# Sixteen-head attention in a four-layer kernel: queries projected from split operands that are streamed by head, their parts made in the layer-0 feed-forward

## What is computed

```python
# layer 0, feed-forward: a router, a shared and an expert branch
shared_out = relu(x @ W_up.T) @ W_down.T
moe_out = sum(softmax(top2(x @ W_gate.T))) * (x @ W_expert)
# layer 2, attention: 16 heads of 128; x is 512 wide, the context 256
q = rmsnorm((x @ Wq).reshape(B, S, 16, 128)) * gq
k = rmsnorm((ctx @ Wk).reshape(B, S, 16, 128)) * gk
v = (ctx @ Wv).reshape(B, S, 16, 128)
attn = softmax(einsum("bqhd,bkhd->bhqk", q, k) / sqrt(128))
out = einsum("bhqk,bkhd->bqhd", attn, v).reshape(B, S, 2048) @ Wo
```

## Time and profile before

| | us |
|---|---|
| median of 3 runs | 3641.05 |
| lowest, highest | 3634.16, 3655.15 |
| the profiled execution, its own time | 3635.72 |
| its span | 3633.9 |

### The profile page before, as it was taken

How to read it: one execution, slowest core, us unless ns; L and a number is a source line. 1 busy time by engine, 2 the same in 40 slices (tenths; PEclk the granted TensorE clock), 3 DMA queues, 4 the chain that set the end, 5 groups by cost and what they waited for, 6 DMA issues and landing times. The chain is left out here.

```text
span 3633.9 us, 43465 instructions
## 1 busy us (share of the span) xinstructions
PE 3207.4 (88%) x14597; PEld 1930.8 (53%) x14628; DVE 2598.7 (72%) x3488; ACT 1806.3 (50%) x3413; POOL 1401.9 (39%) x956
## 2 busy tenths in 40 slices
PE   6868888999996888799999999999999878997995
PEld 2337644333333555455555555555555456785763
DVE  6864679877765888377777877777777755665786
ACT  4644333666663445355555556556655332664220
POOL 1121178000000000166666667766666634223540
PEclk9978999999998999899999999999999888998998
DMA  3026736222218100244544454445454345665311
GB/s 127 37 110 228 265 120 164 59 57 58 62 29 175 29 1 1 82 163 152 176 151 158 161 165 167 157 152 167 154 165 136 104 190 200 239 250 189 139 70 58
DMA packets 229735, 478.69 MB, mean 132 GB/s; under 512 B 36224, under 2 KB 69632, under 8 KB 213649
## 3 DMA queue, kind: packets, MB, share of 16 engines
q1 hardware_dynamic: 223280, 459.19, 39.2%
q0 software_dynamic: 6240, 16.81, 1.3%
HBM read 387.51 MB, written 92.06 MB: 132 GB/s over the span
## 5 line engine op out<-in xcount | busy, mean ns | idle before, releaser
L2341 POOL TENSOR_TENSOR l2x_inflow<-l2x_dtu,l2x_rows_b 128x512 f32<-128x512 f32 x256 | 432.3, 1689 | 332.7 <-DVE l2x_state L2230 311.0
L178 POOL TENSOR_TENSOR ln_work<-ln_work,minus_half 128x4 f32<-128x4 f32 (+1 forms) x34 | 33.3, 978 | 1055.4 <-DVE ln_work L166 1055.3
L2230 DVE TENSOR_TENSOR_SCAN l2x_state<-l2x_decay,l2x_inflow 128x512 f32<-128x512 f32 x256 | 384.6, 1502 | 17.0 <-ACT l2x_decay L2104 17.0
L1300 DVE TENSOR_REDUCE l1x_mx<-psum 128x2 f32<-128x1024 f32 x256 | 308.2, 1219 | 96.0 <-PE psum L1142 94.5
L2044 ACT ACTIVATE l2x_probs<-psum,l2x_soft,l2x_norms 128x512 f32<-128x512 f32 x256 | 195.7, 775 | 321.3 <-DVE l2x_soft L2168 321.3
L2357 POOL TENSOR_TENSOR l2x_y_sum<-l2x_y_sum,l2x_state 128x512 f32<-128x512 f32 x224 | 340.6, 1521 | 33.0 <-DVE l2x_state L2239 33.0
L1257 ACT ACTIVATE l1x_split<-psum 128x1024 f32<-128x1024 f32 x256 | 262.2, 1025 | 154.5 <-PE psum L1142 154.5
L126 PE MATMUL psum<-l2x_probs_t,l2x_v_tok 128*128 128x512 f32 x512 | 238.5, 609 | 32.0 <-ACT l2x_probs_t L212 26.0
L2239 DVE TENSOR_TENSOR l2x_state<-l2x_state,l2x_rows_c 128x512 f32<-128x512 f32 x256 | 251.8, 984 | 6.7 <-issue 0.3
L126 PE MATMUL psum<-l2x_xt,l2x_wq 128*128 128x512 f32 x512 | 230.9, 595 | 7.8 <-issue 6.3
L126 PE MATMUL psum<-l2x_kt,l2x_qt 128*128 128x512 f32 x512 | 231.3, 595 | 4.0 <-ACT l2x_probs L2044 4.0
(11 more groups left out here) (446 smaller groups left out, 7311.6 us busy)
## 6 DMA issues: line engine op xcount, KB each, us to landing
l2x_rows_b<-l3x_xd_dram SPq DMA_DIRECT2D x256, 256.0 KB, 3.6
l2x_rows_c<-l3x_xd_dram SPq DMA_DIRECT2D x256, 256.0 KB, 3.5
l2w_raw<-l_w SPq DMA_DIRECT2D x38, 1024.0 KB, 6.3
l2x_wkv<-l2x_kv_dram SPq DMA_DIRECT2D x32, 1024.0 KB, 7.0
l2w_raw<-l_w SPq DMA_DIRECT2D x38, 512.0 KB, 4.6
l1x_heads_dram<-l1x_stage SPq DMA_DIRECT2D x32, 512.0 KB, 3.3
l2x_wq<-l_wq SPq DMA_DIRECT2D x16, 1024.0 KB, 7.2
l2x_wo<-l_wo SPq DMA_DIRECT2D x16, 1024.0 KB, 5.4
```

Source lines behind the costliest of these rows:

```text
L1300: main.drain(dve.tensor_reduce(mx[:, gg % 2, :, j, t], g["psum"][:, b:b + 2, :], AX.X, ALU.max), f"m{n}_0", banks=2)
L2230: dve.tensor_tensor_scan(state[:, s % KEPT, :], decay[:, s % 3, :], inflow[:, s % 3, :], 0.0, ALU.mult, ALU.add).then_inc(scan_done, 1)
L2341: pool.tensor_tensor(inflow[:, s % 3, :], dtu[:], rows_b[:, s % 3, :], ALU.mult).then_inc(inflow_ready, 1)
```

## The change

Queries of `l2_xattn` are made as split products, 12 fp32r matmuls a head in place of 4 float32 ones. For that `l0_ffn` makes eight more splits, p = 12 to 19, two heads of `l2_wq` each, into a new `q_dram`. There are then 20 splits, and one follows every piece from m = 3 to m = 22, where before one followed every second piece. `s_parts` stays single. POOL's order changes with it.

In `l2_xattn` the weights come from `q_dram` head by head, 512 KB a head with both parts, into two slots of `wq`: 2 MiB a unit, where it was 1 MiB. SP issues heads 2 and 3 of unit u + 1 at its steps n = 7 and 8 of unit u, and heads 0 and 1 of unit u + 2 at n = 11 and 13, each once the head that last read the slot is done. `xt` has two parts: ACT copies all four banks (hi) and DVE subtracts for all four (lo), where each copied two. To make room, `KEPT` is 6, `y_sum` has one slot (POOL's first sum of a unit now waits until DVE has read the sum of the unit before), and the keys' squares go into `q_sq`, so that ACT waits for the sums of squares (`ssq`) of the unit before. On the host `l2_wq` is laid out by head; this is outside the time.

```diff
--- before.py
+++ after.py
@@ l0_ffn: SP
             def split_load(p):
                 k, b = divmod(p, 4)
-                src = a[("ctx_t", "l2_wk", "l2_wv")[k]].rearrange("(c p) n -> p c n", p=P)
+                if p < 12:
+                    src = a[("ctx_t", "l2_wk", "l2_wv")[k]].rearrange("(c p) n -> p c n", p=P)[:, :, b * S:(b + 1) * S]
+                else:
+                    src = a["l2_wq"][2 * (p - 12):2 * (p - 11)].rearrange("h p n -> p h n")
                 if p >= 2:
                     sp.wait_ge(s_lo, p - 1)
-                sp.dma_start(s_raw[:, p % 2], src[:, :, b * S:(b + 1) * S]).then_inc(s_in[p % 2], 16)
+                sp.dma_start(s_raw[:, p % 2], src).then_inc(s_in[p % 2], 16)
...
+                    sp.dma_start(g["q_dram"][2 * (p - 12):2 * (p - 11)].rearrange("h p r n -> p r h n"),
+                                 s_parts[:].bitcast(F32)).then_inc(s_stored, 16)
 
             def split_step(m):
-                if m >= 3 and m % 2:
-                    split_store((m - 3) // 2)
-                    if (m - 3) // 2 + 2 < 12:
-                        split_load((m - 3) // 2 + 2)
+                if 5 <= m < SPLITS + 5:
+                    split_store(m - 5)
+                    if m - 3 < SPLITS:
+                        split_load(m - 3)
...
-            sp.wait_ge(s_stored, 12 * 16)
+            sp.wait_ge(s_stored, SPLITS * 16)
@@ l0_ffn: ACT
             def pieces(i, part):
                 for m in range(6 * i + 2 * part, 6 * i + 2 * part + 2):
                     (absolute if m < 12 else ternary)(m)
-                split_round(3 * i + part)
+                    if 3 <= m < SPLITS + 3:
+                        split_round(m - 3)
@@ l0_ffn: POOL
-                split_rest(3 * i)
-                split_rest(3 * i + 1)
+                for p in range(max(6 * i - 3, 0), 6 * i + 1):
+                    split_rest(p)
                 ln.pool(pool, i)
-                split_rest(3 * i + 2)
+                for p in range(6 * i + 1, min(6 * i + 3, SPLITS)):
+                    split_rest(p)
@@ l2_xattn
-KEPT = 8
+KEPT = 6
...
-            jobs += [(f"xt{(u + 1) // G2}_{c}", "act" if c % 2 else "dve") for c in range(DC)]
+            jobs += [(f"xt{(u + 1) // G2}_{c}", "dve") for c in range(DC)]
...
-        wq, wo = [sb(n, [P, DC, D]) for n in ("wq", "wo")]
+        wq, wo = sb("wq", [P, 2, 2, DC, P], F32R), sb("wo", [P, DC, D])
-        ctx_t, xt = sb("ctx_t", [P, 2, CC, S], F32R), sb("xt", [P, DC, S])
+        ctx_t, xt = sb("ctx_t", [P, 2, CC, S], F32R), sb("xt", [P, 2, DC, S], F32R)
-        k_sq, q_sq = sb("k_sq", [P, S]), sb("q_sq", [P, 4, S])
+        q_sq = sb("q_sq", [P, 4, S])
-        y_sum = sb("y_sum", [P, 2, S])
+        y_sum = sb("y_sum", [P, S])
...
+            def query_weight(u, h):
+                if u < NU:
+                    if u or h >= 2:
+                        ring.wait_filled(sp, 0, f"q{u}_{h - 2}" if h >= 2 else f"q{u - 1}_{h + 2}")
+                    sp.dma_start(wq[:, h % 2].rearrange("p r c n -> p (r c n)").bitcast(F32),
+                                 g["q_dram"][u % G2 * 4 + h].rearrange("p r n -> p (r n)")).then_inc(wq_in[h % 2], 16)
...
-                    if n == 15 and u + 2 < NU:
-                        ring.wait_filled(sp, 0, f"q{u + 1}_3")
-                        weight(wq, "l2_wq", u + 2, wq_in)
+                    if n in (7, 8) and u + 1 < NU:
+                        query_weight(u + 1, n - 5)
+                    if n in (11, 13) and u + 2 < NU:
+                        query_weight(u + 2, (n - 11) // 2)
@@ l2_xattn: PE
-                    pe.wait_ge(wq_in, (u + 1) * 16)
-                    ring.wait_for(pe, 0, free=f"q{u}_{h}", drained=[f"xt{u // G2}_{c}" for c in (2, 3)])
-                    ring.fill(product(pe, bank(f"q{u}_{h}"), [(wq[:, c, h * P:(h + 1) * P], xt[:, c, :])
-                                                              for c in range(DC)]))
+                    pe.wait_ge(wq_in[h % 2], (2 * u + h // 2 + 1) * 16)
+                    ring.wait_for(pe, 0, free=f"q{u}_{h}", drained=[f"xt{u // G2}_{DC - 1}"])
+                    ring.fill(split_product(pe, bank(f"q{u}_{h}"), [
+                        ([wq[:, h % 2, k, c, :] for k in range(2)], [xt[:, k, c, :] for k in range(2)])
+                        for c in range(DC)]))
@@ l2_xattn: ACT
-                    for c in (1, 3):
+                    if u:
+                        ring.wait_filled(act, 0, f"q{u - 1}_3")
+                    for c in range(DC):
...
-                        copy(act, "act", ring, job, xt[:, c, :], bank(job))
+                        act.activation(xt[:, 0, c, :], bank(job), ACT.Copy).then_inc(x_hi, 1)
...
+                    if n == "k" and u:
+                        ring.wait_filled(act, 0, f"ssq{u - 1}")
...
-                                act.activation(k_sq[:, cols], bank(f"k{u}_{t}")[:, cols], ACT.Square,
+                                act.activation(q_sq[:, t, cols], bank(f"k{u}_{t}")[:, cols], ACT.Square,
@@ l2_xattn: DVE
-                    for c in (0, 2):
+                    if u:
+                        ring.wait_filled(dve, 0, f"q{u - 1}_3")
+                    for c in range(DC):
...
-                        copy(dve, "dve", ring, job, xt[:, c, :], bank(job))
+                        dve.wait_ge(x_hi, u // G2 * DC + c + 1)
+                        ring.drain(dve.tensor_tensor(xt[:, 1, c, :], bank(job), xt[:, 0, c, :].bitcast(F32),
+                                                     ALU.subtract), job)
@@ l2_xattn: POOL
                 if n == 1:
-                    since(pool, y_read, u - 1)
+                    since(pool, y_read, u)
```

More of the change, by code:

```diff
@@ L1834, in l2_xattn @@
         b_in, c_in = [[sem(f"{n}_in{k}") for k in range(3)] for n in "bc"]
+        wq_in = [sem(f"wq_in{k}") for k in range(2)]
         ln = LayerNorm(g, sem)
@@ L1902, in _ @@
             weight(wo, "l2_wo", 0, wo_in, rows=True)
-            ring.wait_filled(sp, 0, "q0_3")
-            weight(wq, "l2_wq", 1, wq_in)
+            for h in (2, 3):
+                query_weight(0, h)
+            for h in (0, 1):
+                query_weight(1, h)
             ring.wait_filled(sp, 0, f"v0_{ST - 1}")
@@ L2244, in skip_term @@
                     tile = u_in[:, u % 2, :]
-                    dve.scalar_tensor_tensor(tile, tile, g["skip"][:, u % G2:u % G2 + 1], y_sum[:, u % 2, :], ALU.mult,
+                    dve.scalar_tensor_tensor(tile, tile, g["skip"][:, u % G2:u % G2 + 1], y_sum[:], ALU.mult,
                                              ALU.add).then_inc(y_read, 1)
@@ L2348, in add_state @@
                 s = u * NS + n
-                total = y_sum[:, u % 2, :]
+                total = y_sum[:]
                 pool.wait_ge(gathered, s + 1)
                 if n == 1:
-                    since(pool, y_read, u - 1)
+                    since(pool, y_read, u)
                     pool.tensor_tensor(total, state[:, (s - 1) % KEPT, :], state[:, s % KEPT, :], ALU.add
@@ L3716, in layout @@
                "hadamard": had}
-    arrays |= {"l2_wq": i["L2_xattn_Wq"], "l2_wk": i["L2_xattn_Wk"], "l2_wv": i["L2_xattn_Wv"], "l2_wo": i["L2_xattn_Wo"],
+    heads = i["L2_xattn_Wq"].reshape(DC, P, H2, P).transpose(2, 1, 0, 3).reshape(H2, P, DC * P)
+    arrays |= {"l2_wq": heads, "l2_wk": i["L2_xattn_Wk"], "l2_wv": i["L2_xattn_Wv"], "l2_wo": i["L2_xattn_Wo"],
                "l2_gq": i["L2_xattn_gq"], "l2_gk": i["L2_xattn_gk"]}
```

16 lines of the change are left out of this document (10 added, 6 removed).

## The result

| | before | with the change |
|---|---|---|
| median, us (13 runs each) | 3641.05 | 3663.53 |
| lowest, highest | 3632.24, 3655.15 | 3653.34, 3668.62 |
| the profiled execution: span | 3633.9 | 3658.5 |

The ratio is 1.0062, 95% interval 1.0051 to 1.0074: slower by 22.5 us, where 11 were forecast. The direction and the range held; the size did not, and the two halves of the sum were off in different ways.

The account below looks back on a forecast made before the run. PE was taken as busiest, but each attention unit as tied to a chain through ACT and DVE. Layer 0 +20 and attention -9 gave +11 us on 3641, forecast 3652 us, range 3626 to 3674.

Parts of the forecast that it names:

- The pace of a split: Layer 0: one split's cycle on the single `s_parts`, landing included, takes 9.5 us in batch 0 and 8 elsewhere.
- The way of the sums: Layer 0, batch 1: SP sends and reads back the sums before storing a split; sixth rounding at about 355, batch 2 +8.
- POOL's order: Layer 0, batches 2 and 3: POOL's layer-norm power stands behind the rest of one more split, about 6 us later each.
- my upper bound: Layer 0: +35 us, with landings of 7.4 us at each and every split.
- Queries 0 and 1 kept nothing: Attention, ahead of value 0: both queries' savings turn into a longer PE wait for ACT's copies, 0 us kept.
- Query 2 keeps 0.12 us: Attention, ahead of turn 2: PE starts 0.2 us behind ACT's last exponential, so about 0.12 us of the saving is kept.
- The new-x units keep nothing: Attention units 3, 7, 11: extra ACT copies (1.09 us) and DVE subtractions (1.26 us) eat the kept time.
- Rival 3: Attention: longer waits at value 0 bring the low clock, 2 to 3.4 us a unit, some +30, 3682 us; chance 0.05.
- The edits that I had at nothing: Attention: streaming by head, `KEPT` at 6, one `y_sum` and keys' squares in `q_sq` were put at no cost.
- Rival 1: Attention: PE is the bound and waits shrink with it, so the whole 41 us come, 3620 us; chance 0.12.
- Rival 4: Layer 0: its cost is hidden by PE's slack there, leaving -9 alone, 3632 us; chance 0.08.
- Rival 2: Layer 0 costs +33 with landings of 7.4 us and over, attention keeps only 5: +28, 3669 us; chance 0.20.

Follow-up runs that it names:

- buffers_and_filled: The changed kernel with two slots of `s_parts` and useless matmuls filling PE's wait ahead of value 0: 3625.11 us, ratio 0.9971 to the kernel before.

## Why the prediction was right or wrong

**The pace of a split: right.** I had 8 us a cycle in batch 1, and 9.5 in batch 0. Roundings stand at 292.14 and 300.69 in batch 0 and at 338.44 and 346.99 in batch 1: 8.55 us in both, with landings of about 5. The landings in a chain are nearer the shortest of before (3.8) than its median (7.4); why the old kernel's were longer, at a DMA share of 0.58 to 0.74 against 0.63 to 0.82 now, was not traced. The Trainium skill (DMA: Bandwidth & Descriptors, section Anatomy of one DMA) has 2 us and 436 GB/s, fitted to DMAs that GpSimd issues, where SP issues these; the estimate from it is 4.4 us for 1 MiB, and the 4.5 at the least and 5.3 at the median of the changed kernel agree better than the 7.4 of the earlier trace rows did.

**Layer 0, mis-sized: +36.8 for the +20 of the sum.** One term was too small, and one was not in the sum. *The way of the sums* I had as a delay of the sixth rounding to about 355, so +8 for batch 2's copies of x; they came at 363.42, +15.2. The walk had the rounding ahead of it 5 us too early (341.8 for 346.99), and it gave the store that follows the sums an ordinary landing, where it took 10.2 us beside the copy of 768 KB. *POOL's order* I had at 6 us in each of batches 2 and 3. Batch 2 took 64.9 us for 55.1, +9.8, and batch 3 63.7 for 51.8, +11.8. In the rows shown DVE was ready 10.91 us before 474.63, at 463.7; the rounding came only at 470.03, behind a landing, and after it the subtraction and the power took 3.4 us more. But with the power put first the two batches took 60.9 and 56.9 us: POOL's order is worth 4.0 and 6.8 us, near the 6 that I had. *Not in the sum* are the other 5 to 6 us in each of these batches. They were there with the power first, and nearly so with two slots (59.9 and 56.6 us, though 55.9 and 56.3 in `buffers_and_filled`); their cause stays open, as said above. The measured +36.8 is beyond even my upper bound, +35, and that bound stood on landings of 7.4 us, which did not occur.

**The attention's total, right; its parts, wrong.** -9 was forecast, -12.5 came (-10 by the medians). That they are so near is luck, since it is made otherwise. (The most that could be kept was 64 x 0.63 = 40.3 us, where I had written 41.)

- From its start to the next start a query took 3.43 us before. Now it takes 3.20 where float32 work stands ahead of it, and the float32 product ahead of it takes 3.03 in place of 3.43; the two together save 0.63 us, as computed. The Trainium skill (FP8 and Floating Point Precision, section TensorE Precision Notes) counts four passes for true FP32; three of four would be 2.57 us, an estimate that the rows do not bear out (3.43 - 0.63 = 2.80).
- Queries 0 and 1 kept nothing: right. PE's wait at value 0 went from 1.65 to 2.29 us, and a wait at turn 0 appeared (9 waits became 16). In sum 33.0 us, where I had written 46: query 0's part went into turn 0, and in units 2, 6, 10 and 14 the wait fell to 0.9 us, because query 1 itself met the low level of the clock there: 4.23 to 4.30 us in place of 2.87 (from 1776.63 to 1780.86 in unit 2, with a granted clock of 0.67 from 1777 to 1781). That cost nothing, since it was taken from the wait.
- *Query 2 keeps 0.12 us*: this step failed. I read the 0.2 us between ACT's last exponential and turn 2 as a meeting, though PE's row showed no wait there. The maxima ahead of those exponentials stand on DVE behind a scan step and its product, and DVE was busy there, not waiting for PE. In the old kernel they began 3.68 us after score 2 (1927.39 against 1923.71); in the changed kernel 2.74 (2045.27 against 2042.53):

```profile
2040.98 0.69 DVE L2209 TENSOR_TENSOR l2x_ot<-psum,l2x_inv_b 128x512 f32<-128x512 f32 x1 [0.70 <-PE psum L126]
2041.59 2.14 DVE L2262 TENSOR_TENSOR_SCAN l2x_state<-l2x_decay,l2x_inflow 128x512 f32<-128x512 f32 x1
2043.76 1.58 DVE L2271 TENSOR_TENSOR l2x_state<-l2x_state,l2x_rows_c 128x512 f32<-128x512 f32 x1
2045.27 2.47 DVE L2190 TENSOR_REDUCE l2x_soft<-psum 128x1 f32<-128x512 f32 x4
```

```profile
2042.53 3.60 PE L126 MATMUL psum<-l2x_kt,l2x_qt 128*128 128x512 f32 x8
```

  Counted from score 2, the chain came 0.94 us earlier: since PE now waits longer ahead of value 0, DVE had done its scan work by then and even waited 0.70 us for PE, as the first row shows. So 0.63 us was kept and 0.5 us of slack was left. That padding query 2 counted in full agrees.
- *The new-x units keep nothing*: not seen either. From the value 0 before to their own they take 85.0 us in all three, where it was 85.8, 87.0 and 85.3.
- So about 15 x 1.26 = 19 us were kept on queries 2 and 3. *Rival 3, at 0.05, happened, with 11.6 of its 30 us*: the longer wait brought the low level of the clock at value 0 in 7 units, -11.6 of the gain. At the same time turn 3, which runs in what `ssq` leaves of the clock, got faster: over 14 units it took 33.0 us in place of 39.3. 19 - 11.6 + 6.4 = 13.8, beside 12.5 measured; the rest was not traced. Two errors of mine, query 2 and the clock, nearly cancelled: the total was right by luck.

The edits that I had at nothing (`KEPT`, the one `y_sum`, the streaming by head) show little cost: POOL waited 57.1 us for `u_in` at its first sums, nobody waited for POOL's sums, and DVE waited 4.8 us, in three places, for POOL's `inflow`, which it had not before. PE waited for a streamed head once, 3.4 us.

Rival 1 would have given -41; PE's 95% busy share was no bound, as its waits said. Rival 4 fell with the marks of layer 0. Rival 2's 3669 came nearer to the measured 3663.53 than my 3652, and its +33 in layer 0 nearer to +36.8 than my +20, but its mechanism, landings of 7.4 us and over, was not the one.
